# GNN and attention layer on one core: a rebuilt second norm, table rows written per block, and a first normalising shared by two engines

## What is computed

```python
xn = layernorm(x)
h  = relu(batchnorm(xn @ w1.T + b1)) @ w2.T + b2
gcn[dst] += (h @ w_gcn.T)[src] * dinv[src] * dinv[dst]      # with self loops
mix = linear_attention(xn, 8 heads) @ wo + bo
x1 = x + gcn + b_gcn + mix
xf = layernorm(x1)                                          # the second norm
g  = xf @ W_gat                      # 16 columns: 4 heads x 4 experts
a_src, a_dst = (g * att_src).sum(-1), (g * att_dst).sum(-1) # 4 + 4 columns
# softmax over 131072 edges and the self loops, by destination; top 2 of 4 experts
out = x1 + sum over experts e of gate[e] * (gelu(xf @ W1[e] + b1[e]) @ W2[e] + b2[e])
```

## Time and profile before

| | |
|---|---|
| median of 3 runs | 4779.59 us (4776.38 to 4796.87) |
| profiled execution, its own time | 4790.88 us |
| its span, first to last instruction | 4789.0 us |
| PE, DVE, ACT, POOL busy | 77%, 54%, 18%, 64% |
| mean granted TensorE clock | 0.843 |
| first stage, first gather stage, second norm, second gather stage | to 271, to 2746, to 2996, to about 4455 us |

### The profile page before, as it was taken

How to read it: one execution, slowest core, us unless ns; L and a number is a source line. 1 busy time by engine, 2 the same in 40 slices (tenths; PEclk the granted TensorE clock), 3 DMA queues, 4 the chain that set the end, 5 groups by cost and what they waited for, 6 DMA issues and landing times. The chain is left out here.

```text
span 4789.0 us, 44151 instructions
## 1 busy us (share of the span) xinstructions
PE 3688.3 (77%) x13162; PEld 2442.9 (51%) x13162; DVE 2604.3 (54%) x6218; ACT 880.5 (18%) x1738; POOL 3085.5 (64%) x3019
## 2 busy tenths in 40 slices
PE   3667888888798998787887564799999999700377
PEld 1355555455555555555555354466666666500255
DVE  5946776666666556666666364134334333312476
ACT  2653222222100000000000011222222223200232
POOL 2515777777776776777777500777777777777630
PEclk7989999999887998777677655899999999955689
DMA  6645444444454664333333765444444334322588
GB/s 178 188 98 152 129 130 132 130 130 130 125 154 132 182 177 131 89 91 89 92 91 89 71 193 137 132 114 113 138 115 113 117 106 138 97 63 63 114 209 196
DMA packets 262492, 606.63 MB, mean 127 GB/s; under 512 B 88254, under 2 KB 144369, under 8 KB 256893
## 3 DMA queue, kind: packets, MB, share of 16 engines
q0 software_dynamic: 124496, 304.94, 24.1%
q1 hardware_dynamic: 137772, 299.02, 22.2%
HBM read 447.85 MB, written 155.88 MB: 126 GB/s over the span
## 5 line engine op out<-in xcount | busy, mean ns | idle before, releaser
L1039 POOL DMA_INDIRECT g_rows<-table,gcn_srcT x1664 | 1758.2, 1057 | 568.0 <-issue 485.7
L1109 PE MATMUL g_ps<-g_rows,g_hot 128*125 128x256 f32 x3328 | 1064.3, 456 | 337.4 <-issue 229.6
L1902 POOL DMA_INDIRECT n_rows<-gtab,so_own x1122 | 1095.6, 977 | 341.9 <-issue 341.9
L1394 DVE TENSOR_TENSOR acc<-acc,g_ps 125x256 f32 x1664 | 696.4, 419 | 691.6 <-PE g_ps L1109 565.6
L1109 PEld LDWEIGHTS g_ps<-g_rows,g_hot 128*125 128x125 f32 x3328 | 685.8, 223 | 622.8 <-issue 410.0
L1842 PE MATMUL p_ph<-f_xfT,f_w 128*128 128x500 f32 x1344 | 576.7, 585 | 64.2 <-DMA f_xfT<-xfT_d 64.2
L1848 PE MATMUL p_py<-f_w,f_hh 128*125 128x256 f32 x2688 | 590.4, 379 | 0.0
L1848 PEld LDWEIGHTS p_py<-f_w,f_hh 128*125 128x125 f32 x2688 | 504.5, 188 | 101.1 <-issue 27.4
L2045 DVE TENSOR_TENSOR p_ob<-p_py,p_xb 125x512 f32<-125x512 f32 x168 | 115.6, 691 | 699.0 <-PE p_py L1848 698.6
L1842 PEld LDWEIGHTS p_ph<-f_xfT,f_w 128*128 128x128 f32 x1344 | 256.4, 191 | 348.6 <-issue 343.5
L2073 ACT ACTIVATE f_hh<-p_ph,f_b 128x500 f32<-128x500 f32 x336 | 221.4, 677 | 616.4 <-PE p_ph L1842 616.1
(11 more groups left out here) (338 smaller groups left out, 4329.8 us busy)
## 6 DMA issues: line engine op xcount, KB each, us to landing
o_d<-p_ob SPq DMA_DIRECT2D x21, 1920.0 KB
z_ob<-o_d SPq DMA_DIRECT2D x21, 1920.0 KB
g_rows<-table,gcn_srcT POOLq DMA_INDIRECT x1664, 3.0
n_rows<-gtab,so_own POOLq DMA_INDIRECT x1122
gout<-n_o SPq DMA_DIRECT2D x33, 408.0 KB, 2.5
xnT_d<-a_xnT SPq DMA_DIRECT2D x25, 500.0 KB
m_area<-xnT_d SPq DMA_DIRECT2D x25, 500.0 KB, 3.8
qT_d<-m_area SPq DMA_DIRECT2D x25, 500.0 KB, 3.1
```

What stands on the lines that cost most here:

```text
L1039: pool.indirect_dma_start(out=rows[:, g % RING, j], out_offset=None, in_=K.table, in_offset=bass.IndirectOffsetOnAxis(ap=K.gcn_srcT[:, 4 * ...
L1109: mm = pe.matmul(ps[q, p % 4, b], hot[:, g % 4, 2 * j + b], rows[:, g % RING, 2 * j + b], start=True, stop=True, skip_group_check=True)
L1394: dve.tensor_tensor(a, a, ps[q, p % 4, b], ALU.add).then_inc(add_s, 1)
L1902: pool.indirect_dma_start(out=rows[:, c % 3, j], out_offset=None, in_=K.gtab, in_offset=bass.IndirectOffsetOnAxis(ap=K.gat_src[:, c * W + ...
```

## The change

- In `second_norm` everything is written anew, without hardware loops: three buffers for `pre` and for `x1`; SP's order is, for each k, the store of x1 of block k, the load of block k+3, the store of the transposed block k-1, and the table rows of block k-2. ACT normalises all four tiles of a block, with scale 1/sigma and bias -mean/sigma that DVE prepares (`off`). The products with att_src and att_dst are folded into W_gat once, so that PE gives all 24 columns. ACT copies them into a `wide` buffer that POOL has cleared, and each block writes whole table rows of 512 bytes, four in a row per partition.
- For that the table's order changes: node t*125 + p is now row p*100 + t. `lists` turns K.gat_src and K.gat_head into the new numbers with three more DVE instructions each.
- `first_half` no longer writes the blank. Of the four tiles of a block DVE normalises two and ACT two (`normalise` in ACT's stream, after its copies of the block before).

```diff
 first_half, SP:
                 def load(k):
                     if k >= 3:
-                        sp.wait_ge(xn_s, (k - 2) * SUB)
+                        sp.wait_ge(xn_s, (k - 2) * (SUB // 2))
+                        sp.wait_ge(xna_s, (k - 2) * (SUB // 2))
...
-                sp.wait_ge(blank_s, 1)
-                sp.dma_start(K.gtab.rearrange("(t p) f -> p t f", p=TN)[:, :, TROW:TWIDE],
-                             blank[q].unsqueeze(1).to_broadcast([TN, NT, TWIDE - TROW])).then_inc(blank_s, 16)
 first_half, ACT:
+                def normalise(k):
+                    s = k % 2
+                    act.wait_ge(off_s, k + 1)
+                    if k >= 2:
+                        act.wait_ge(turned, (k - 1) * KC)
+                    for j in range(SUB // 2, SUB):
+                        act.activation(xn[q, s, j], xin[q, k % 3, j], ACT.Identity, bias=off[q, s, j:j + 1],
+                                       scale=rs[q, s, j, 0:1]).then_inc(xna_s, 1)
...
                     for ch in range(KC):
                         act.wait_ge(turned, k * KC + ch + 1)
                         act.copy(xnT[:, k % 2, ch], ptr[:, ch, 0:BN]).then_inc(xnT_s, 1)
+                    if k + 1 < NB:
+                        normalise(k + 1)
 first_half, DVE:
+                    dve.scalar_tensor_tensor(off[q, s], mv[q, s, :, 0], -1.0, rs[q, s, :, 0], ALU.mult, ALU.mult
+                                             ).then_inc(off_s, 1)
-                    for j in range(SUB):
+                    for j in range(SUB // 2):
                         dve.tensor_scalar(xn[q, s, j], xin[q, k % 3, j], mv[q, s, j, 0:1], rs[q, s, j, 0:1],
                                           ALU.subtract, ALU.mult).then_inc(xn_s, 1)
 gather_mix, DVE, lists:
+                    for at, of in ((K.gat_head[:, 0:1], odd[:]), (K.gat_src, K.opens.bitcast(I32))):
+                        then(dve.tensor_scalar(of, at, 1.0 / TN, 0.5 / TN - 0.5, ALU.mult, ALU.add))
+                        then(dve.tensor_scalar(at, at, float(NT), None, ALU.mult))
+                        yield
+                        then(dve.scalar_tensor_tensor(at, of, float(1 - TN * NT), at, ALU.mult, ALU.add))
+                        yield
 second_norm, SP:
+                for k in range(RING):
+                    load(k)
+                for k in range(NB + 2):
+                    if k < NB:
+                        sp.wait_ge(x1_s, (k + 1) * SUB)
+                        rows_in_two(sp, K.x1_d[k], x1[:, k % RING], out_1[k % RING])
+                        if k + RING < NB:
+                            load(k + RING)
+                    if 0 <= k - 1 < NB:
+                        sp.wait_ge(xfT_s, k * KC)
+                        sp.dma_start(K.xfT_d[k - 1], xfT[:, (k - 1) % 2]).then_inc(out_f[(k - 1) % 2], 16)
+                    if k >= 2:
+                        sp.wait_ge(row_s, k - 1)
+                        rows_in_two(sp, by_part[k - 2], wide[:, k % 2].rearrange("p j f -> p (j f)"), out_g[k % 2])
 second_norm, DVE:
+                statistics(0)
+                dve.wait_ge(w_s, 16 * 3)
+                for a in range(2):
+                    dve.tensor_tensor(prod[:, a], wg[:, :, 0:GW], att[:, a].unsqueeze(1).to_broadcast([P, KC, GW]), ALU.mult
+                                      ).then_inc(fold_s, 1)
+                dve.wait_ge(fold_s, 2)
+                for a in range(2):
+                    dve.tensor_reduce(wg[:, :, GW + a * GH:GW + (a + 1) * GH],
+                                      prod[:, a].rearrange("p c (h e) -> p c h e", h=GH), AX.X, ALU.add).then_inc(fold_s, 1)
+                for k in range(NB):
+                    if k + 1 < NB:
+                        statistics(k + 1)
+                    scales(k)
 second_norm, ACT:
+                roots(0)
+                roots(1)
+                normalise(0)
+                act.wait_ge(clear_s, 1)
+                for k in range(NB):
+                    if k + 2 < NB:
+                        roots(k + 2)
+                    if k + 1 < NB:
+                        normalise(k + 1)
+                    copies(k)
+                    if k:
+                        rows(k - 1)
+                rows(NB - 1)
```

More of the change, by code:

```diff
@@ L438, in first_half @@
         pb = m.ps("a_pb", [P, 512])
[L439 to L442, removed]
+        (w_s, both_s, bias_s, off_s, xna_s, st_s, mv_s, eps_s, root_s, rec_s, xn_s, turned, xnT_s, h_s, hT_s, stat_s, deg_s, v) = (m.sem("a_" + s) for s in (
+             "w", "both", "bias", "off", "xna", "st", "mv", "eps", "root", "rec", "xn", "turned", "xnT", "h", "hT", "stat", "deg", "v"))
         (dst_s, src_s, after_s, short_s, rows_out, pay_s, pairs_out, pad_s, edge_s, fell, spread_s, head_s, met_s, row_s, side_s,
@@ L1702, in store @@
[L1702 to L1709, removed]
@@ L1724, in _, with load @@
-                sp.wait_ge(S["trow"], 1)
-                sp.dma_start(K.gtab.rearrange("(t p) f -> p t f", p=TN)[:, :, 0:TROW], trow[0:TN]).then_inc(S["out"], 16)
-                sp.wait_ge(S["out"], 16)
+                def load(k):
+                    if k >= RING:
+                        sp.wait_ge(x1_s, (k - RING + 1) * SUB)
+                    rows_in_two(sp, pre[:, k % RING], K.pre_d[k], in_p[k % RING])
+                sp.dma_start(wg[:, :, 0:GW], A.W_gat.rearrange("(c p) o -> p c o", p=P)).then_inc(w_s, 16)
@@ L1728, in _ @@
+                for s in range(RING):
+                    sp.wait_ge(out_1[s], 32 * ((NB + RING - 1 - s) // RING))
+                for s in range(2):
+                    sp.wait_ge(out_f[s], 16 * ((NB + 1 - s) // 2))
+                    sp.wait_ge(out_g[s], 32 * ((NB + 1 - s) // 2))
+            @block.gpsimd
+            def _(pool):
+                pool.memset(wide[:], 0.0).then_inc(clear_s, 1)
             @block.vector
             def _(dve):
-                dve.sem_inc(S["x1"], 2 * SUB)
@@ L1777, in _ @@
-                for a, out in ((0, trow[0:TN, :, GW:ROW]), (1, trow[0:TN, :, ROW:TROW])):
-                    dve.tensor_tensor(prod[0:TN], hg[0:TN], att[0:TN, a].unsqueeze(1).to_broadcast(shape), ALU.mult
-                                      ).then_inc(S["prod"], 1)
-                    dve.wait_ge(S["prod"], a + 1)
-                    dve.tensor_reduce(out, prod[0:TN].rearrange(v4, h=GH), AX.X, ALU.add).then_inc(S["row"], 1)
-                    dve.wait_ge(S["row"], a + 2)
-                dve.sem_inc(S["trow"], 1)
+                        dve.wait_ge(st_s, k * SUB + j + 1)
@@ L1803, in _, with roots, normalise @@
-                roots(0, 0)
-                blocks(act, body)
+                def roots(k):
+                    act.wait_ge(eps_s, k + 1)
+                    act.activation(rs[q, k % 2, :, 1], rs[q, k % 2, :, 0], ACT.Sqrt).then_inc(root_s, 1)
+                def normalise(k):
+                    s = k % 2
+                    act.wait_ge(off_s, k + 1)
+                    if k >= 2:
+                        act.wait_ge(turned, (k - 1) * KC)
+                    for j in range(SUB):
+                        act.activation(xf[q, s, j], x1[q, k % RING, j], ACT.Identity, bias=off[q, s, j:j + 1],
+                                       scale=rs[q, s, j, 0:1]).then_inc(xf_s, 1)
@@ new lines, in copies, with rows @@
+                def copies(k):
+                    s = k % 2
+                    if k >= 2:
+                        act.wait_ge(out_f[s], 16 * (k // 2))
+                    for c in range(KC):
+                        act.wait_ge(turned, k * KC + c + 1)
+                        act.copy(xfT[:, s, c], ptr[:, s, c, 0:BN]).then_inc(xfT_s, 1)
+                def rows(k):
+                    s = k % 2
+                    if k >= 2:
+                        act.wait_ge(out_g[s], 32 * (k // 2))
+                    act.wait_ge(h_s, k + 1)
+                    act.copy(wide[q, s, :, 0:TROW], ph[q, s, 0:SUB * TROW].rearrange("p (j o) -> p j o", j=SUB)
+                             ).then_inc(row_s, 1)
```

152 lines of the change are left out of this document (57 added, 95 removed).

## The result

The changed kernel takes 4672.54 us (median of 4 runs, 4666.96 to 4678.85) against 4786.39 (4 runs, 4776.38 to 4796.87): a ratio of 0.976, 95% interval 0.973 to 0.979, so 114 us faster by the medians. Predicted were 4655 us and 124 us. The profiled executions differ by 111.9 us of span (4789.0 to 4677.1).

| stretch | before, us | after, us | difference | predicted |
|---|---|---|---|---|
| start to the first instruction after the first stage (first `r_bn`) | 270.9 | 215.0 | -55.9 | -57.7 |
| from there to the second norm's first instruction | 2478.8 | 2498.1 | **+19.3** | +1 |
| second norm, to the next stage's first issue | 246.3 | 173.2 | -73.1 | -67.6 |
| the rest | 1793.0 | 1790.8 | -2.2 | 0 |

A forecast was written before the change was run, and what follows sets the result against it. Stages each end in a wait of all engines, so time saved in one comes off the end. Gains 45.2 + 12.5 + 67.6 less 1 make 124.3 us, taken from the median 4779.59: 4655 us, range 4638 to 4690.

The forecast's parts named there:

- Blank gone: First stage: without the blank's store ahead of block 3's load, VectorE's wait for x goes; gain 45.2 us.
- First normalising shared: First stage: VectorE gives two of four normalisings to ScalarE, blocks 6.76 instead of 7.32 us; gain 12.5 us.
- Second norm's loop: Second norm: buffers, store order and lighter VectorE work bring blocks from 7.58 to 6.2 us; gain 33 us.
- Its beginning: Second norm's start: added folds of W_gat and ScalarE's work after the scales delay the first transposes; loss 1 us.
- Its end: Second norm's end: from the last copy to the next stage 5.9 us instead of 41.5; gain 35.6 us.
- The indices: First gather stage: VectorE's added index instructions cost 1 us, bounds 0 and 4.5, as POOL paces the stage.
- Rival A: Second norm: TensorE's clock rises once the holes are gone, 10 us more gain, 4645 us; chance 6%.
- B: Second norm: transfers bind, waits return under another name, blocks of 7.3 us, 4681 us; chance 14%.
- C: First stage gives less: ScalarE's order binds (4668 us) or the hole is only partly the blank's (4678); chance 12%.
- D: Attention gather: the new row order makes each gather longer; at 0.15 us more, 4823 us; chance 1%.

The follow-up runs named there:

- e1: Changed kernel with the memset and the store of zeros into the table's padding put back ahead of the first stage's fourth load: 4725.7 us.
- e4: Changed kernel with the edits of e1 and e2 together, so the first stage is as in the kernel before: 4734.2 us.
- e2: Changed kernel with the first stage's normalising back on VectorE alone, four tiles a block, blank store still out: 4692.7 us.
- e11: Changed kernel with two buffers instead of three in the second norm and its normalising back on VectorE: 4679.6 us (1 run).
- e12: Changed kernel with the remapping moved into the second norm and TensorE transposing the next block ahead of this block's products: 4659.0 us.
- e3: Changed kernel without the remapping of the gathers' lists, table in its old row order, wide rows stored as 512-byte pieces: 4656.4 us.

## Why the prediction was right, and where it was not

The time, 4672.5, lies within the range of 4638 to 4690 and 17.5 above the point. Some 10 us of that are the gain (113.9 us by the medians for 124.3), some 7 the median of the kernel before, which with one run more is 4786.4 and not 4779.6. That the gain comes so near is luck in part: the second norm gave 5.5 us more than forecast and the rest of the span 2.2, and both stand against 18.3 us lost in the first gather stage. Term by term:

- *Blank gone*, 45.2: 46.6 by e1, 45.0 by e4 against e2. Right in mechanism and size.
- *First normalising shared*, 12.5: 10.8 by e2. The block came out at 6.72 for the predicted 6.76, and block 24 starts 13.5 us earlier than in e2 (175.96 and 189.45). The end of the stage takes 2.7 of it back, where the step had put 1.5: VectorE waits 3.0 us for ScalarE's bias copies (0.5 in e2) and 8.1 for its signs (7.4). ScalarE's two cost more than I took: four in a row take 2.07 us in the second norm (mean 590 ns, two operands per row), where the earlier trace rows with one such operand had 1.71. The Trainium skill, "ScalarE: Activation LUTs", section "What ACT_TABLE_LOAD costs", gives 186 ns + 0.833 ns per column + 93 ns per pointer operand, and 93 ns of overlap: estimates of 585 ns for one and 2.06 us for four. This trace agrees: 590 ns and 2.07 us.
- *Second norm's loop*, 33: 37.0, at 6.04 us a block instead of 6.2, the bound given as TensorE's chain alone. Of the reasons ("both pre and x1 now have three buffers, and SP issues x1's store before it waits for the copies") the first is refuted by e11 and only the second is left, argued and not shown; VectorE's lighter load, which I worked out with care, bought nothing. "So the 51.7 us of waiting go" was wrong as well: VectorE waits for loads instead, 47.4 of 120 us, and it did not matter, since TensorE no longer waits for VectorE's rows.
- *Its beginning*, -1: 0.0 (16.65 us from first issue to first transposes, 16.66 before). *Its end*, 35.6: 36.2, read from the two timelines; no run puts the old end back.
- *The indices*, -1 with bounds 0 and 4.5: **this step failed**. It cost 15 to 16 us in its stretch (95.3 to 96.4 without, 111.6 with, twice). The step priced the added instructions by their own length and by POOL's slack over the whole stage. What it left out: they, and the later place of the steps behind them, hold up VectorE's additions, for which TensorE waits; with them TensorE has 41 to 55 us at half clock in G where it had 24 to 27 without, and POOL waits for it.
- The other 3 us of the 19.3 and the 2.2 of the rest lie within what the stages scatter.

Rival A is refuted: the clock stayed at 0.50 with TensorE busy 106 of 120 us, and 108 in e12. So the rule of the Trainium skill, "TensorE: Matmul & The Clock Gate", part 1, that a busy engine gets its full clock, did not hold here, for work made of transposes and narrow products. B's sign came and its price did not: VectorE waits for loads in nearly every block (20 waits in 120 us), but TensorE is not held up by it; at 5.5 us a block it begins to be (e12). C did not come: blocks of 6.72 us, and the hole was all the blank's; the first stage fell 1.8 us short of its 57.7. D is refuted by 1.28 us a gather.

## What to carry to other kernels

Price an instruction added to a shared engine by who waits behind it, and look at the granted clock in the very stretch: here 3 us more of VectorE's work, with the later place of what stood behind it, went with 27 us more at half clock and cost 15, and a place with slack (the second norm) took the same work for nothing. When a change bundles buffers, a split of work and a new order of transfers, undo them alone and together: here one buffer was needed only because of the split, and neither had made the loop faster. In a queue served in order, try to put the transfer whose data are ready ahead of the one that must still wait; here that is the likely gain, and it still lacks a run of its own.

## What the runs showed of the hardware

How long the first gather stage takes follows TensorE's time at half clock. The 14 profiles reach from 656 us at half clock with 2314.7 us of gathers (e3) to 754 with 2357.9 (e2); a straight line through all of them has 0.40 us per us, with a correlation of 0.96. Gathers 704 to 896 took 288 to 315 us in kernels whose instructions there are the same, and the gathers outside G, 2219 to 2252 us, go up and down with them (correlation 0.93). In the second norm the clock stayed at half with TensorE busy 0.89 of the time in the changed kernel and 0.90 in e12. 5.2 MB of zeros in pieces of 416 bytes kept the load behind them back for 46 us, with the DMA engines at 0.38 and 99 GB/s.
